# Two-block transformer kernel on one core: rounding of weights, start of softmax attention, start of the gated stages

## What is computed

```python
x = x + 0.5 * _L0_ffn_ref(_layernorm(x), ...)      # two routed experts, one shared (hidden 1024)
x = x + _L0_attn_ref(_layernorm(x), ...)           # linear attention, 16 heads of 16
x = x + 0.5 * _L0_ffn_ref(_layernorm(x), ...)
x = x + 0.5 * _L1_ffn_ref(_layernorm(x), ...)      # gated, 704 wide, inputs and weights rounded to FP4
x = x + _L1_attn_ref(_layernorm(x), ...)           # softmax attention, q = k = v
x = x + 0.5 * _L1_ffn_ref(_layernorm(x), ...)

def fp4_quant_dequant(x):
    xb = x.reshape(shape[:-1] + (shape[-1] // BLOCK, BLOCK))         # BLOCK = 16
    scale = jnp.maximum(jnp.max(jnp.abs(xb), axis=-1, keepdims=True) / 6.0, 1e-12)
    idx = jnp.searchsorted(_MID, jnp.abs(xb / scale))
    return (_GRID[idx] * jnp.sign(xb) * scale).reshape(shape)

def _L1_attn_ref(x, W_qkv, W_o):
    qkv = (x @ W_qkv.T).reshape(b, n, H, DH).transpose(0, 2, 1, 3)
    score = softmax(einsum('bhif,bhjf->bhij', qkv, qkv) / SQRT_D, axis=-1)
    return einsum('bhij,bhjf->bihf', score, qkv).reshape(b, n, F) @ W_o.T
```

## Time and profile before

| what | value |
| --- | --- |
| median of 3 runs | 3193.49 us (3186.46 to 3194.48) |
| the profiled execution, its own time | 3204.97 us |
| its span, first to last instruction | 3203.2 us |
| mean granted TensorE clock | 0.97 |
| busy PE, DVE, ACT, POOL | 3026.5, 2449.4, 2051.0, 563.9 us |
| stages by the trace, us from the span's start | routed 0 to 431, linear attention to 745, routed to 1166, gated to 1432, softmax attention to 2936, gated to 3203 |

### The profile page before, as it was taken

How to read it: one execution, slowest core, us unless ns; L and a number is a source line. 1 busy time by engine, 2 the same in 40 slices (tenths; PEclk the granted TensorE clock), 3 DMA queues, 4 the chain that set the end, 5 groups by cost and what they waited for, 6 DMA issues and landing times. The chain is left out here.

```text
span 3203.2 us, 62253 instructions
## 1 busy us (share of the span) xinstructions
PE 3026.5 (94%) x24412; PEld 2004.5 (63%) x24412; DVE 2449.4 (76%) x4830; ACT 2051.0 (64%) x3762; POOL 563.9 (18%) x628
## 2 busy tenths in 40 slices
PE   7999979987999979988999999999999999997998
PEld 6899868776889969984343333334333333343998
DVE  7433558865533479975988999999999999983987
ACT  5544534444544546641677888887888888876665
POOL 3322325543322332220000000000000000001222
PEclk9999989998999989997799999999999999998999
DMA  4211120002211100002303011110303030000000
GB/s 135 78 44 33 56 61 2 2 2 70 85 40 43 42 29 1 1 3 92 41 28 57 12 25 19 19 24 2 42 2 42 2 42 2 2 2 1 14 19 23
DMA packets 60258, 99.39 MB, mean 31 GB/s; under 512 B 7568, under 2 KB 43584, under 8 KB 57280
## 3 DMA queue, kind: packets, MB, share of 16 engines
q1 hardware_dynamic: 53632, 78.10, 11.2%
q0 software_dynamic: 6336, 17.31, 1.7%
HBM read 64.84 MB, written 30.41 MB: 30 GB/s over the span
## 5 line engine op out<-in xcount | busy, mean ns | idle before, releaser
L2282 DVE TENSOR_REDUCE smxp<-psum 128x1 f32<-128x512 f32 x2048 | 1259.0, 681 | 43.1 <-PE psum L2133 41.5
L2242 ACT ACTIVATE spr<-psum 128x512 f32<-128x512 f32 x2048 | 1114.6, 596 | 270.1 <-PE psum L2157 223.1
L2133 PE MATMUL psum<-sks,sqs 48*128 48x512 f32 x2048 | 785.6, 465 | 11.8 <-DMA sqs<-q_parts 11.0
L2157 PE MATMUL psum<-sqs,sks 50*128 50x512 f32 x2048 | 755.3, 453 | 0.0
L2174 PE MATMUL psum<-spr,sv 128*32 128x256 f32 x8192 | 659.4, 393 | 11.0 <-ACT sot L2249 8.7
L2133 PEld LDWEIGHTS psum<-sks,sqs 48*128 48x128 f32 x2048 | 323.1, 190 | 434.1 <-issue 385.3
L2174 PEld LDWEIGHTS psum<-spr,sv 128*32 128x32 f32 x8192 | 163.2, 108 | 381.9 <-ACT spr L2242 292.1
L2157 PEld LDWEIGHTS psum<-sqs,sks 50*128 50x128 f32 x2048 | 302.9, 186 | 16.0 <-issue 9.3
L1859 POOL MEMSET fhqb<- 128x64 f32 x3 | 0.3, 153 | 1501.9 <-POOLq L2046 1501.9
L542 PE MATMUL psum<-w_b,hsb_hi 128*128 (+1 forms) x1056 | 193.1, 281 | 2.2 <-DVE hsb_lo L799 2.2
L542 PE MATMUL psum<-w_a,hsa_hi 128*128 (+1 forms) x1056 | 192.3, 280 | 1.3 <-DVE hsa_lo L799 1.3
(11 more groups left out here) (421 smaller groups left out, 5877.5 us busy)
## 6 DMA issues: line engine op xcount, KB each, us to landing
sks<-q_parts SPq DMA_DIRECT2D x42, 256.0 KB, 9.4
sqs<-q_parts SPq DMA_DIRECT2D x42, 256.0 KB, 19.7
q_parts<-spart SPq DMA_DIRECT2D x16, 512.0 KB, 2.8
x<-in_L_attn_x_dram SPq DMA_DIRECT2D x8, 512.0 KB, 7.2
yoa<-in_L_ffn_w_dram SPq DMA_DIRECT2D x16, 256.0 KB
xga<-f_sorted_a SPq DMA_DIRECT2D x8, 512.0 KB, 3.8
f_routed_a<-yoa SPq DMA_DIRECT2D x8, 512.0 KB, 2.9
yob<-in_L_ffn_w_dram SPq DMA_DIRECT2D x16, 256.0 KB
```

The source lines that it names most:

```text
L2133: e.matmul(bank(what), QS[n % 2][rows, pr, q0:q0 + P], KS[n % 2][rows, pr, jc * GW:(jc + 1) * GW], start=True, stop=True, tile_position=(H ...
L2157: e.matmul(out, KS[n % 2][rows, pr, jt * P:(jt + 1) * P], QS[n % 2][rows, pr, ic * GW:(ic + 1) * GW], start=True, stop=True, tile_position ...
L2242: e.activation(PR[j % 2][:, HEAD[i], :], src, ACT.Exp, scale=float(DH) ** -0.5).then_inc(*done.up)
L2282: e.tensor_reduce(out[:, r // (2 * GT * IC), r // (2 * IC) % GT, r // 2 % IC, r % 2:r % 2 + 1], bank(what), AX.X, ALU.max).then_inc(*pm_fr ...
```

## The change

In all stages: `load_table` issues a one-column activation, so that a set of tables is loaded at that place. Linear attention: weights are rounded with `QuantiseMax`, its steps spread over several places i (`vector_steps`, `magnitude_at`, `product_at`), two sets of temporaries for chunks; `w_down` is turned in four batches of three pieces. Gated stages: the low parts of the weights are made on VectorE between the roundings of the first tiles, and ScalarE turns to `high_x(0)` and `low_x(0)` behind the first tile. Softmax attention: the turned tiles of sequence 0 are kept in AO's memory (`XT0`), the plan first makes half 0 of every group's projection and its stacks, then values 0 to 3, and the other twelve values and the four halves 1 come one by one behind every fourth maximum; the maxima of unit 0 go by key column, each column waiting for its own stack (`first_in`).

```diff
+        def load_table(e, func):
+            e.activation(table_in[:], eps[:], func)
...
+                DOWN = 4 + 2 * CH
+                DP = C1 // 2
+                WS = DOWN + 15
...
+                def quantise_w(j):
+                    if j < CH:
+                        a, c = divmod(j, C1)
+                        rows, nbk = rows_of(j), D // QB
+                        tmp = (qtmp[0][:, :, j % 2 * nbk:(j % 2 + 1) * nbk], qtmp[1][:, :, j % 2 * D:(j % 2 + 1) * D])
+                        q = QuantiseMax(gu[0:rows, a, c, :], D, rows, tmp, guq[j % 2][0:rows], wq_sum, wq_ok)
+                    else:
+                        q = QuantiseMax(dn[:, j - CH, :], H1, P, qtmp, dnq[:], wq_sum, wq_ok)
+                    return q.events(j, wq_y, wq_abs)
+                def chunk_at(i, first):
+                    k, odd = divmod(i - first, 2)
+                    return k if 0 <= k < CH and not odd else None
+                def vector_steps(i):
+                    if chunk_at(i, 5) is not None:
+                        return chunk_at(i, 5), (4, 5)
+                    if chunk_at(i, 4) is not None:
+                        return chunk_at(i, 4), (0, 1, 2, 3)
+                    return {DOWN: (CH, (0,)), DOWN + 1: (CH, (1, 2, 3)), DOWN + 3: (CH, (4,)), DOWN + 4: (CH + 1, (0,)),
+                            DOWN + 5: (CH, (5,)), DOWN + 7: (CH + 1, (1, 2, 3)), DOWN + 9: (CH + 1, (4,)),
+                            DOWN + 11: (CH + 1, (5,))}.get(i)
+                def magnitude_at(i):
+                    return CH if i == DOWN + 2 else CH + 1 if i == DOWN + 8 else chunk_at(i, 4)
+                def product_at(i):
+                    return CH if i == DOWN + 6 else CH + 1 if i == DOWN + 12 else chunk_at(i, 6)
                 def turned_at(i):
                     if i in (1, 3):
                         return "plain", i // 2, 0
-                    if 7 <= i < 7 + 2 * CH and i % 2:
-                        return "chunk", (i - 7) // 2 // C1, (i - 7) // 2 % C1
-                    if 6 + 2 * CH <= i < 6 + 2 * CH + C1:
-                        return "down", 0, i - 6 - 2 * CH
-                    if 7 + 2 * CH + C1 <= i < 7 + 2 * CH + 2 * C1:
-                        return "down", 1, i - 7 - 2 * CH - C1
+                    j = chunk_at(i, 7)
+                    if j is not None:
+                        return "chunk", j // C1, j % C1
+                    if i in (DOWN + 7, DOWN + 8):
+                        return "down", 0, (i - DOWN - 7) * DP
+                    if i in (DOWN + 13, DOWN + 14):
+                        return "down", 1, (i - DOWN - 13) * DP
...
+                            if i is not None and magnitude_at(i) is not None:
+                                quantise_w(magnitude_at(i)).scalar(e)
...
+                                if t == T - 1:
+                                    load_table(e, ACT.Sqrt)
...
+                            j, steps = vector_steps(i)
+                            if steps[0] == 0:
+                                if j < CH:
+                                    e.wait_ge(*gu_in[j // C1](2))
+                                else:
+                                    e.wait_ge(*dn_in(1))
+                                if 2 <= j < CH:
+                                    e.wait_ge(*wq_ok(j - 1))
+                            if steps[0] == 1:
+                                e.wait_ge(*wq_ok(j))
+                            q = quantise_w(j)
+                            for step in steps:
+                                if step in (1, 5):
+                                    q.at = dv.now()
...
+                            j = product_at(i)
+                            e.wait_ge(*wq_sum(j + 1))
+                            if 2 <= j < CH:
+                                e.wait_ge(*misc_in(misc_use["w", 7 + 2 * (j - 2)] + 1))
+                            if j == CH + 1:
+                                e.wait_ge(*misc_in(misc_use["w", DOWN + 8] + 1))
+                            quantise_w(j).gpsimd(e)
...
                         normal(1)
+                        load_table(e, ACT.Silu)
                         quantise_x(0).scalar(e)
+                        e.activation(wu[0][:], wuT[:], ACT.Copy).then_inc(*whi_ok.up)
+                        high_x(0)
+                        low_x(0)
                         normal(2)
                         quantise_x(1).scalar(e)
-                        e.activation(wu[0][:], wuT[:], ACT.Copy).then_inc(*whi_ok.up)
+                        e.activation(wd[0][:], wdT[:], ACT.Copy).then_inc(*whi_ok.up)
                         normal(3)
                         quantise_x(2).scalar(e)
-                        e.activation(wd[0][:], wdT[:], ACT.Copy).then_inc(*whi_ok.up)
-                        high_x(0)
-                        low_x(0)
                         for t in range(T + LAG):
...
+                            if t == T and not store:
+                                load_table(e, ACT.Sqrt)
...
+                        low_weights(0, wg, wgT)
                         for t in range(AHEAD):
                             made_x[t % 2] = quantise_x(t)
                             for i in range(6):
                                 step_x(t, i)
+                            if t == 0:
+                                low_weights(1, wu, wuT)
+                        low_weights(2, wd, wdT)
...
-                        low_weights(0, wg, wgT)
                         end_x(0)
                         end_x(1)
-                        low_weights(1, wu, wuT)
                         end_x(2)
-                        low_weights(2, wd, wdT)
...
+                def part_buffer(b, g, o):
+                    return g % 2 if b == 0 else o
+                def part_number(b, g, o):
+                    return o * IC + g if b == 0 else (b * IC + g) * KD + o
+                def parts_out(b, g, o):
+                    return part_out[part_buffer(b, g, o)]((o * IC + g) // 2 + 1 if b == 0 else b * IC + g + 1)
+                def first_keys():
+                    for t in range(TB + 2):
+                        if t < TB:
+                            yield ("norm", 0, t)
+                        if t >= 2:
+                            yield ("turn", 0, t - 2)
+                        g, i = divmod(t - 2, GT)
+                        if g >= 0 and i == GT - 1:
+                            yield ("parts", 0, g, 0)
+                            if g:
+                                yield ("stack", 0, g - 1)
+                    yield ("stack", 0, IC - 1)
...
+                def max_of(m):
+                    u, r = divmod(m, MPU)
+                    if u == 0:
+                        jc, pr, i, a = r // (2 * GT * NPR), r // (2 * GT) % NPR, r // 2 % GT, r % 2
+                    else:
+                        pr, i, jc, a = r // (2 * GT * IC), r // (2 * IC) % GT, r // 2 % IC, r % 2
+                    return u, r, pr, i, jc, a
                 def plan():
-                    for g in range(IC):
-                        yield from itertools.islice(project_steps(0), 14 * g, 14 * (g + 1))
-                        yield ("stack", 0, g)
+                    yield from first_keys()
+                    for t in range(GT):
+                        yield ("value", 0, t)
+                    late = iter([("value", 0, t) for t in range(GT, TB)] + [("parts", 0, g, 1) for g in range(IC)])
                     for m in range(MPU + LEAD):
                         if m > MPU and m % MPU == BEHIND:
                             yield ("extremes", m // MPU - 1)
                         yield ("max", m)
+                        if m % 4 == 3:
+                            yield from itertools.islice(late, 1)
...
+                                o = g * HG * DH // P
+                                for last in range(max(first + count - 2, 0), first + count):
+                                    e.wait_ge(*parts_out(b, last, o))
...
+                                if u == 0 and r % (MPU // IC) == 0:
+                                    e.wait_ge(*first_in[jc](4 * NPT))
...
+                                if b and t and t % GT == 0:
+                                    e.wait_ge(*made(("value", b, t - 1)))
...
+                                if u == UNITS - 1:
+                                    load_table(e, ACT.Sqrt)
```

More of the change, by code:

```diff
@@ L1354, in weights @@
                                 turned(("w", i))
-                                e.activation(wdT[0:rows, c, a * P:(a + 1) * P], misc[0:rows, 0:P],
-                                             ACT.Copy).then_inc(*misc_free.up)
+                                full = min(DP, C1 - 1 - c)
+                                m = e.activation(wdT[:, c:c + full, a * P:(a + 1) * P],
+                                                 misc[:, 0:full * P].rearrange("p (c n) -> p c n", n=P), ACT.Copy)
+                                if full < DP:
```

(5 more changed lines are left out.)

103 lines of the change are left out of this document (40 added, 63 removed).

## The result

The changed kernel takes **3145.08 us** in the median of 4 runs (3140.56 to 3150.74), the kernel before 3190.39 in 4 runs beside them: a ratio of 0.9855, 95% interval 0.9838 to 0.9872, so 45.3 us less. The forecast was 3143.0 with a range of 3126 to 3160. The profiled execution took 3150.74 us, its span 3149.0; against the profiled execution of before that is 54.2 less, of which 8.6 lies in the two routed stages, whose code is the same (846.6 against 838.0 us together). So this is a matter of this execution or of its chip, where the kernel before is some 15 us faster too, and no gain.

The account below looks back on a forecast made before the run. PE, busy 94% of the span, was taken as the bound, so only its waits or work at another engine's pace could give time back. Terms summed to -50.5 us, from a median of 3193.49 to 3143.0, range 3126 to 3160.

Parts of the forecast that it names:

- Chunks: Linear attention, gate and up weight rounding: no change, as PE fills the 8.29 us period; a gain excluded.
- `w_down` rows: Linear attention, rounding of w_down spread over iterations: eight iterations take 67.4 us against 85.2, -17.8 us.
- Sqrt load in linear attention: Table load moved ahead of the routed stage's start into ACT's idle time in linear attention: -1.0 us.
- Start of the gated stages: Both gated stages: weight subtracts move from POOL to DVE, so the first left product comes earlier; -6.4 us each.
- Tail of the first gated stage: Early Sqrt load delays a copy PE waits for by 1.4 us, one more half-clock stretch likely: +2.4 us.
- Opening: Softmax attention: half the projections before the first maximum, the rest later; first score at 1514.4 against 1534.64, -20.3 us with Sqrt load.
- the prediction's own sign of being wrong: Softmax attention: a first score less than 15 us earlier than 1534.6; other signs were PE waits in chunks, half-clock first maxima.
- Last load: Second gated stage's start: 1.28 us of table load saved, 0.2 given back where ACT's end copy waits; -1.1 us.
- the clock is low among the first maxima: Softmax attention: late work among maxima runs at half clock, 12 us back, giving 3155 us; chance 0.12.
- The clock stays high into the main loop: Softmax attention: late work keeps PE at full clock, saving 9.5 us of half-clock start, giving 3133.5 us; chance 0.2.
- the bound of the gated stages' start: Rival: DVE becomes the gated stages' bound, or Abs delays linear attention; +9 and +5, 3152 to 3157 us; chance 0.1.
- the reordering: Softmax attention: rival that it does nothing, SP's stacks still ending last and chunks filling the gaps; 3163 us; chance 0.03.

Follow-up runs that it names:

- e2: The changed kernel with linear attention's old weight rounding, seven steps in one iteration; 3173.88 us, ratio 0.9896 to the kernel before.
- e4: The changed kernel with all three early Sqrt loads taken out, so each stage's std loads the table; 3153.25 us, ratio 0.9836 to the kernel before.
- e8: The changed kernel without the early Sqrt load in the first gated stage's tail, the other two kept; 3151.01 us, ratio 0.9824 to the kernel before.
- e1: The changed kernel with softmax attention's old opening and old unit order; 3172.07 us, ratio 0.9891 to the kernel before.
- e5: The changed kernel with each group's parts issued two tiles later in softmax attention's opening; 3149.82 us, ratio 0.9822 to the kernel before.
- e6: The changed kernel with late projections and values behind every fifth maximum instead of every fourth; 3173.43 us, ratio 0.9886 to the kernel before.

## Why the prediction was right, point by point

The total, 3143.0 for 3145.1, is nearer than its terms, and in part by luck. The saving was forecast at 50.5 us and measured at 45.3; of the 5.2 between them 3.1 do not show in the total, as the kernel before took 3190.4 us beside it and not the 3193.5 from which the forecast was taken off. The terms missed by up to 5.4 us: by stages 3.0 more than forecast in linear attention and 0.6 in gated b, 5.4 less in the opening and 3.1 in the main loop, and they partly cancel.

1. *Chunks, 0.* Wrong by -3.1: the iterations with chunks went from 8.28 to 8.09 us, and the one of 9.29 to 7.93. The step that failed is "a gain is excluded, PE being full". A row "8.29, all PE" is no proof of that. In such iterations of before the four turns of `aos` hold PE 0.58 to 0.66 us (once 0.80) from start to start, in the new kernel 0.49, and in e2, with the old rounding, 0.57 to 0.66 (once 0.79) again: short waits, covered by modelled ends, and most of the 0.19. In the iteration of 9.29 the hold is 1.87 us, and there the wait shows, 1.21 us for DVE's `aaoT_lo`; that the short ones are for it too is likely and not shown. The Trainium skill, "Perfetto Trace Analysis", section "Per-instruction lifecycle: what the profiler-reported window actually captures", says that TensorE's reported end is estimated from the instruction's size. The rows agree: busy equals span in both kernels, and the spans differ.
2. *`w_down` rows, -17.8.* Measured -17.8 from start to start over the eight iterations that end at the last of the twelve transposes (85.4 to 67.6; forecast 67.4). Right, and at full clock; the two iterations that were to keep a wait, forecast at 9.8 and 9.2 us, took 10.2 and 9.5.
3. *Sqrt load in linear attention, -1.0.* From the last tile's turn to the next std 48.8 us became 48.0; the twelve profiles with the early load have 48.0 to 48.8, the two without it 48.8 and 49.5 (before, e4): 0 to -1.6. Right in kind. On the load itself, the trace shows 1.28 us and the next activation 0.01 to 0.02 behind it, in every place. The 1.38 of drain that the Trainium skill gives ("ScalarE: Activation LUTs", "What ACT_TABLE_LOAD costs") cannot be seen: in the last stage, where nothing covers the load, moving it saved 1.1 and not 2.7. (The prediction's sum by that page is wrong in itself: 8.0 for 3.6 is 4.4 more, so about -55 and not -53.)
4. *Start of the gated stages, -6.4 each.* Undoing it costs 6.1 and 6.0. First left product forecast at std + 7.9, measured + 7.9. Right. The stretch has not gone but changed sides: beside DVE's third subtract a product of POOL (L245) takes 2.07 us where it else takes 0.62.
5. *Tail of the first gated stage, +2.4.* The wait grew by 1.49 for a forecast 1.4. One more stretch at half clock came too, as forecast: 6.8 us in the tail, before 3.4. That e8 gives 4.2, still inside the bounds, is because its tail has no such stretch, though PE waits there as long as in before (2.38 and 2.36 us). Over the profiles with the early load the tail has 3.4 to 10.2 us at half clock, so chance moves this term by some 3 us. With the 1.28 that leave this stage the forecast for gated a was -5.3, and so it came.
6. *Opening, -20.3.* The largest miss. From std to first score, where 19.0 were due (the load's 1.28 lies ahead of std), it is 13.6 in the first profile, 13.6 to 17.7 over the profiles with the same opening, and 15.0 against e1. Counted from std, the prediction's own sign of being wrong came for this part, a first score less than 15 us earlier (13.6, or 14.9 with the load), and the first maximum came 21.0 us earlier with the load and not some 25. The step that failed is the group cadence of 5.0 us, with its product at "3.70/2 = 1.85". It was 6.6, as a product behind PE's waits runs at 1.2 GHz. The text had the low clock only for the first product. e5 shows that it is this: with the clock held, a group takes 4.2 us (1.8 of the 2.4 less are the product's own) and std to first maximum 23.1, even under the forecast's 26.5. The late work's price was nearly right (6.1 for 5.4), and so was the claim that the stacks no longer hold PE.
7. *Last load, -1.1.* 12.9 to 11.8 from last score to std. Right.

Of the rivals, "the clock is low among the first maxima" never happened in nine profiles of this arrangement, but it is real: one density lower (e6) and it comes, at 19.9 us where 12 were priced. "The clock stays high into the main loop" did not come in the changed kernel: its clock falls before the first score in both profiles. It was argued for by the rule of the Trainium skill, "TensorE: Matmul & The Clock Gate", section "What's actually happening", that the lower state follows an idle window and activity releases it. The trace disagrees on both halves: the clock fell behind 1.64 us of work in 3.40, and did not rise under 55.33 of 58.00. DVE was not the bound of the gated stages' start, by item 4, and the reordering did something, by item 6. The slower case needs over 115 us more at half clock; the time there varied by 26 over all profiles.

## What to carry to other kernels

Price a stretch by the clock that it will run at: a matmul behind two short waits can cost twice its row, and an order that lets products find their inputs ready (e5) can give more than the waits themselves. Fill work for a thin stretch is safest dense and at once behind work that holds the clock; the same fill begun later or spread thinner cost 17 to 20 us in one profile each here. Before a term counts as zero because PE is "all busy", compare starts of the same instructions, and before crediting a few microseconds of a loop to a change, profile the same kernel twice.

## What the runs showed that was not expected

- Two lasting states of the clock for nearly the same work: 51.2 us at 2.4 GHz with PE busy 86%, 58.0 us at 1.2 GHz with PE busy 95%. The second ended with the first product of 128 rows and 512 columns.
- The time until the clock rises in a main loop full of PE work: 8.8 to 32.6 us for one program.
- A subtract of 1408 columns takes 1.63 us on DVE and 3.16 on POOL, and a 16-column DVE step beside POOL's takes 2.29 us instead of 0.17, ending as POOL's does.
- A table load of 1.28 us put into a place where PE already waits cost 4.2 us, over three times its own length, against profiles whose tail kept the full clock.
